# Attention on one core: a maxima item moved ahead of each slot's first score tile, and one more tile of the row sums given to GpSimd in four chunks of eight

## The reference

```python
scores = jnp.einsum('bihd,bjhd->bhij', q, k) * SCALE      # 2 batches, 32 heads, 2048 x 2048, causal
scores = jnp.where(causal, scores, jnp.finfo(scores.dtype).min)
attn = jax.nn.softmax(scores, axis=-1)                    # exp(s - row maximum) / row sum
out = jnp.einsum('bhij,bjhd->bihd', attn, v)
```

## Time and profile before

| | us |
|---|---|
| median of 3 runs | 3619.89 (3619.73 to 3621.58) |
| the profiled execution | 3618.96, its span 3617.1 |
| PE busy | 3496.1 (97%) |
| PEld busy | 2441.7 (68%) |
| DVE busy | 1920.7 (53%) |
| POOL busy | 1560.4 (43%) |
| ACT busy | 1493.0 (41%) |
| mean granted TensorE clock | 0.987 of full |

### The profile page before, as it was taken

One profiled execution on the slowest core, in us unless ns is written; L12 is line 12 of the kernel. 1 busy time (PEld: TensorE's weight loads), 2 busy tenths in 40 slices (PEclk: granted clock), 3 DMA queues, 4 the chain that ended last, 5 costly groups with the idle time before them and its releaser, 6 DMA issues. The chain is left out here.

```text
span 3617.1 us, 63262 instructions
## 1 busy us (share of the span) xinstructions
PE 3496.1 (97%) x26058; PEld 2441.7 (68%) x26058; DVE 1920.7 (53%) x3577; ACT 1493.0 (41%) x1839; POOL 1560.4 (43%) x672
## 2 busy tenths in 40 slices
PE   8999998999999999999999999999969999999999
PEld 7888885555565565565565556556537888888887
DVE  3121217666666666666666666666615666642223
ACT  3111112555555555555555555555542222221111
POOL 0000002867867877787786787787530000000000
PEclk9999997999999999999999999999989999999999
DMA  6343325021111111111111111110026787755553
GB/s 209 117 129 114 110 87 116 23 51 48 34 41 48 44 30 50 47 31 49 48 30 50 48 35 38 48 38 9 12 84 203 230 226 225 214 192 173 177 182 128
DMA packets 248224, 340.69 MB, mean 94 GB/s; under 512 B 55440, under 2 KB 150288, under 8 KB 247952
## 3 DMA queue, kind: packets, MB, share of 16 engines
q1 hardware_dynamic: 247952, 336.87, 31.6%
HBM read 203.08 MB, written 133.17 MB: 93 GB/s over the span
## 5 line engine op out<-in xcount | busy, mean ns | idle before, releaser
L680 DVE TENSOR_REDUCE p_part_max<-p_qm 128x1 f32<-128x512 f32 (+3 forms) x2240 | 1351.6, 667 | 711.0 <-PE p_qm L533 448.7
L503 POOL TENSOR_TENSOR p_psums<-p_psums,p_probs 128x1024 f32<-128x1024 f32 x560 | 1331.9, 2378 | 82.1 <-ACT p_probs L643 2.2
L643 ACT ACTIVATE p_probs<-p_km 128x1024 f32<-128x1024 f32 x896 | 902.9, 1023 | 445.2 <-PE p_km L561 384.2
L533 PE MATMUL p_qm<-p_k_st,p_q_st 96*128 96x512 f32 (+3 forms) x2560 | 911.9, 425 | 14.7 <-DMA p_q_st<-q_hi 10.8
L533 PEld LDWEIGHTS p_qm<-p_k_st,p_q_st 96*128 96x128 f32 x2560 | 483.9, 195 | 244.7 <-DVE p_part_max L680 170.0
L561 PE MATMUL p_km<-p_q_st,p_k_st 97*128 97x512 f32 x1792 | 609.8, 422 | 5.1 <-ACT p_probs L643 5.1
L568 PE MATMUL p_o<-p_probs,p_v 128*32 128x256 f32 (+1 forms) x9216 | 581.3, 371 | 0.0
L499 POOL TENSOR_TENSOR p_psums<-p_probs 128x1024 f32<-128x1024 f32 x95 | 226.4, 2383 | 489.2 <-ACT p_probs L643 489.2
L568 PEld LDWEIGHTS p_o<-p_probs,p_v 128*32 128x32 f32 x9216 | 270.8, 110 | 214.5 <-issue 61.9
L561 PEld LDWEIGHTS p_km<-p_q_st,p_k_st 97*128 97x128 f32 x1792 | 304.0, 190 | 143.8 <-issue 104.2
L41 PE MATMUL p_acc<-p_xT_hi,p_w_hi 128*128 128x512 f32 x640 | 250.2, 391 | 9.6 <-DVE p_w_lo L226 9.6
(11 more groups left out here) (150 smaller groups left out, 4130.1 us busy)
## 6 DMA issues: line engine op xcount, KB each, us to landing
p_q_st<-q_hi SPq DMA_DIRECT2D x128, 256.0 KB, 4.8
p_x_raw<-in_xT SPq DMA_DIRECT2D x64, 256.0 KB, 3.4
q_hi<-p_out_hi SPq DMA_DIRECT2D x64, 256.0 KB, 2.0
q_lo<-p_out_lo SPq DMA_DIRECT2D x64, 256.0 KB, 2.3
p_q_st<-q_lo SPq DMA_DIRECT2D x64, 256.0 KB, 4.4
attended_T<-p_o_raw SPq DMA_DIRECT2D x128, 128.0 KB
p_a_raw<-attended_T SPq DMA_DIRECT2D x32, 512.0 KB, 5.3
p_recip<-reciprocals SPq DMA_DIRECT2D x128, 128.0 KB, 6.9
```

Source lines behind the costliest of these rows:

```text
L503: pool.tensor_tensor(sums[:, :, :], sums[:, :, :], probs[s % PB][:, :, :], ALU.add).then_inc(added, 1)
L533: last = pe.matmul(bank[:, x * keys:(x + 1) * keys], q_st[par][0:ROWS, c, h + x, sub * P:(sub + 1) * P], k_st[par][0:ROWS, j * CK:j * CK + ...
L643: act.activation(tile[:, :, :].rearrange("p h q -> p (h q)"), km[s % 2][:, :, :].rearrange("p a b -> p (a b)"), ACT.Exp, scale=SCALE).then ...
L680: dve.reduce_max(part_max[c][:, h:h + heads, sub, j], qm[bank_of(i)][:, 0:item_width(i)].rearrange("p (h k) -> p h k", h=heads), AX.X).the ...
```

## The change

Two places. In the steady groups `pooled` becomes 2c - (c < 4), so chunks 2 and 3 keep 3 and 5 tiles, and chunks 4 to 7 go from 7, 9, 11, 13 to 8, 10, 12, 14. GpSimd makes 46 additions a group in place of 42, and TensorE four products of ones with a tile fewer in each of these chunks. `LAST_SUMS` is left. And in TensorE's stream the first of the two items that stood behind the first score tile of each slot now stands ahead of it. The streams of VectorE and ScalarE keep their order.

```diff
-    SUMS = Sums([2 * c - 1 if c > 1 else 0 for c in range(NC)])
+    SUMS = Sums([2 * c - (c < 4) if c > 1 else 0 for c in range(NC)])
     LAST_SUMS = Sums([c + 1 if c > 2 else 0 for c in range(NC)])
...
             def group(n, par, placed, plan=SUMS):
                 for sl, (_, steps) in enumerate(SLOTS):
                     for s in steps:
+                        leading = 1 if s == steps[0] else 0
+                        for ahead, i in placed[s][:leading]:
+                            item(n + ahead, (par + ahead) % 2, i)
                         scores(n, par, s)
-                        for ahead, i in placed[s]:
+                        for ahead, i in placed[s][leading:]:
                             item(n + ahead, (par + ahead) % 2, i)
                     if sl > 0:
                         values(n, par, sl - 1, plan)
```

## The result

The changed kernel is slower, and by twice what was forecast: 3756.37 us median (3752.97 to 3757.87) against 3619.81, a ratio of 1.0373 with an interval of 1.0361 to 1.0385. Forecast were 3687 us and a range to 3728. The profiled execution took 3752.97 us, its span is 3751.2.

The account below looks back on a forecast made before the run. GpSimd's queue was taken to bound 94.88 us of the cycle, TensorE the other 35.20. Fourteen cycles at +4.74 us (+66), with group 0 and the last group +67 in all, gave 3687 us, range 3658 to 3728.

Parts of the forecast that it names:

- the first half of its cycle: From chunk 4's first addition to chunk 7's last, GpSimd's queue sets the time: 94.88 us before, about 100.4 forecast.
- the second half: From chunk 7's sum to the next chunk 4, TensorE sets the pace: 35.20 us, less 1.8, plus 1.4 for the clock.
- The prediction's own sign of being wrong: It would be wrong if, among others, chunk 7's sum to the next chunk 4 took under 31 or over 37 us.
- GpSimd's four additions more: Chunks 4 to 7: idle times eaten, 40 additions at 2.515 us make a chain of 100.4 us, 5.5 us more a cycle.
- TensorE's sets of ones: Four sets of 0.43 us less, 1.7 us a group, ahead of the wait for chunk 7; worth nothing on the path.
- The waits: TensorE waits for GpSimd at the sums of chunks 6 and 7, about 4 and 8 us, 150 to 200 us in all.
- the eight leads ahead of it: Items moved first in eight slots ahead of chunk 6's sum: TensorE there earlier by 0.4 us each, 3.2 us.
- The clock: Behind every wait at chunk 7's sum TensorE's clock drops, costing 1.4 us; bounds 0.4 and 2.8 us.
- Rival 2: Clock stays low much longer than 3 us; if all 35 us ran low, 15 us a cycle, about 3890 us; chance 0.03.
- The upper bound of the range: 3728 us for the whole run: the case of a lead winning nothing, with a bit for longer drops.
- The lead: Between chunk 7's sum and chunk 4, item first: 0.4 us for each of five slots, less 0.2, 1.8 us gained a cycle.
- The sum: A cycle of 100.4 + (35.2 - 1.8) + 1.4 = 135.2 us against 130.46, +4.74; fourteen of them, +66.

Follow-up runs that it names:

- the run of the table alone: Against the changed kernel, every item stays behind its score tile; pooled tiles of chunks 4 to 7 still 8, 10, 12, 14: 3754.90 us, ratio 1.0376.
- The run with filler in the wait: Changed kernel plus 32 products of 512 columns, overwritten later, just ahead of TensorE's wait at chunk 7's sum: 3694.55 us, ratio 1.0202.
- the run with dense work there: Changed kernel plus 16 products of 512 columns right behind the product with chunk 7's sum: 3785.76 us, ratio 1.0452.
- the ones with half exponentials: Kernel before with pooled 8, 9, 11, 12 and half the exponential of most slots' first tile left out: 3585.19 us without, 3545.22 us with the lead.
- with filler ahead: Changed kernel plus 24 products of 512 columns ahead of the wait at chunk 7's sum, leaving a 2.1 us wait: 3747.30 us, ratio 1.0322.

## Why the prediction was wrong

Its direction and the first half of its cycle were right. In the second half two terms failed: the loss at the low clock was too small by a factor of about three, which makes 42 of the 69 us missed (fourteen times 3.0), and the lead's gain of 1.8 us a cycle isn't there, which makes 25. The prediction's own sign of being wrong, a second half of over 37 us, is there: the mean is 39.6.

- **GpSimd's four additions more**: forecast 5.5 us a cycle, measured 5.2, chain 100.10 against 100.4; the queue has no idle time, as forecast.
- **TensorE's sets of ones**: worth nothing on the path, as said. The waits were forecast at 4 and 8 us and are 1.4 and 7.7 in the cycle shown (126.7 us in all, where I said 150 to 200). The first was too long because the eight leads ahead of it were counted at 0.4 us each: without any lead, in the run of the table alone, the wait is still 0.9 us in the mean, where it is 1.4 with them, so all eight are worth about 0.4. That the second comes out is luck in part: between the two sums I took 1.6 us off for leads and put 1.4 on for the clock, and in this cycle both are nearly nothing.
- **The clock**: this is the step that failed, and the larger of the two. I took "1.4 us behind every wait", from a spell of some 3 us behind a wait of 1.6 us and from one behind the gap of 7.46 us in the next stage. It costs 4.8 us in the cycle shown and 4.4 in the mean (39.6 against 35.2). Rival 2 named the mechanism and put 3 in 100 on it, with "slot 1 is dense" against it. That sentence was the mistake: the row it leaned on, behind the gap of 7.46 us, has full products back to back, while slot 1 has products of 96 rows with mask products between them. The run with filler in the wait takes 62 us away, so that the loss is the clock's is shown. That the kind of work behind the wait matters has support in the run with dense work there (6.8 us to the end of the spell in place of 10.2, in the mean); it isn't the whole reason, since behind the same slot 1 as work the clock came back early in three cycles before and in some with the table alone. The row of 540 to 600 us, clock 0.60 with PE busy 47 of 60, was the one in hand that showed a long spell under work, and rival 2 drew 3890 from it.
- **The upper bound of the range** was at fault as well: "twice the drop, 2.8" was twice a number I had, not a bound from a row.
- **The lead**: forecast 1.8 us a cycle in the second half, measured 0 (35.28 against 35.20). The run with the lead alone and the ones with half exponentials show what stands in its place: about 1 us that I took for a gain isn't there even with ScalarE out of the way, and the 0.8 that is there ScalarE takes back. In slot 5 I worked out that behind the third score tile all would go in 2.01 us; PEld in order of time in the changed kernel:

```profile
1318.54 0.19 PEld L533 LDWEIGHTS p_qm<-p_k_st,p_q_st 96*128 96x128 f32 x1 [0.41 <-issue]
...
1320.69 0.30 PEld L554 LDWEIGHTS p_km<-p_q_st,p_k_st 97*128 97x128 f32 x2 [0.45 <-ACT p_probs L646]
1321.26 0.10 PEld L556 LDWEIGHTS p_km<-p_mask_k,p_ident_bf 128*128 128x128 bf16 x1 [0.27 <-issue]
...
1323.25 0.16 PEld L568 LDWEIGHTS p_o<-p_probs,p_v 128*32 128x32 f32 x8 [0.25 <-issue]
```

The third tile waits 0.45 us for ScalarE and starts 2.15 us into the slot (before 2.08), and from there to the values it is 2.56 us (before 2.49). Before, this stretch already ran almost at TensorE's own speed, with 0.1 to 0.3 us between loads that no buffer explains ("issue"); I had counted products alone. So in this slot the wait for VectorE was exchanged for one for ScalarE of about the same length, and over the whole span the first falls by 90 us (170.0 to 79.8) and the second grows by 60 (10.7 to 70.6).
- **The sum**: with 4.4 for 1.4 and 0 for 1.8, the prediction's cycle would be 100.4 + 35.2 + 4.4 = 140.0, where 139.67 was measured.

The Trainium skill ("TensorE: Matmul & The Clock Gate", "HAM oscillation — how this bites in real kernels") warns of just this: a stall that comes back in each pass makes each pass start at the low clock. The traces agree: behind each of the fourteen waits of 6.5 to 7.7 us slot 1 takes 6.4 us or more in place of 4.8, and the price is 62 us of 3756, 1.6%. The Trainium skill (the same page, "Part 1: The HAM clock gate") puts the slow start at less than 1% of a typical kernel's span; here it recurs fourteen times, and the measurement decides.

What stays open: what makes a spell short, long or absent behind the same wait and the same work. Waits of 1.6 to 2.0 us left slot 1 alone in 22 of 28 cycles and cost its full price in one; waits of 7.4 to 7.5 gave anything from 5.8 to 8.6 us for it. No run here took the phase of the wait against the chip's own timing apart, nor the filler ahead of a wait from the wait itself.

## What to carry to other kernels

An engine off the critical path with a serial queue has a hard capacity: count its operations between the point where its input starts and the point where another engine waits for the sum, at the pace of its full stretches (here 2.51 us, not 2.38), and give it only what fits; here one tile less in the longest chunk made the kernel faster and one more cost 86 us. A wait of TensorE costs what it stands still plus what the work behind it loses at the low clock, and a row stands for that loss only if both the wait and the work behind it are like those of the case. Where no row has both, take the worst of them as the bound. Before moving work ahead to feed one engine sooner, look which wait of the next engine takes over within the same tenths of a microsecond.

## What the runs showed of the hardware that was not expected

- The loss at the low clock doesn't grow in proportion to the idle time ahead: none at 0.4 us, 1.4 us in 3 of 14 cycles at 1.6, over 4 us in 13 of 14 at 2.1 with filler ahead. But at 1.9 to 2.0 us without filler there was none in 11 of 14, and the full price in one.
- The clock can fall after the work is back (in the run with 14 tiles in chunk 7: 1.00 over the last 3 us of 4.6 us of standing still, 0.53 over the next 3) and then stay low for over 12 us of work.
- Work that computes nothing, put into the wait, made the changed kernel 62 us faster. Giving GpSimd one addition less, so that there is no wait, makes it 24 us faster than the kernel before.
